# Decoder layer with attention, quantised cross product and gated experts: column sums of the context on GpSimd, row sums and two layernorm applications on ScalarE, product terms added to x ahead of the product

## What is computed

```python
x = x + attn(layernorm(x), Wq, Wk_down, Wv_down, Wk_up, Wv_up, Wo)    # 32 heads, 8 key/value heads, causal
x = x + matmul(fake_quant(layernorm(x), s1, z1), fake_quant(ctx, s2, z2))
x = x + ffn(layernorm(x), A_w, B_w, Wq_w, keys)                        # 64 experts of rank 8, the 16 best gated

def fake_quant(x, s, z):
    return (clip(round(x / s + z), 0, 255) - z) * s
```

## Time and profile before

| | us |
|---|---|
| median of 3 runs | 1156.27 (1155.45 to 1157.93) |
| the profiled execution | 1155.61 |
| its span, first to last instruction | 1153.7 |
| PE busy in the span | 1121.5 (97%) |
| DVE busy | 773.4 (67%) |
| ACT busy | 464.1 (40%) |
| POOL busy | 233.7 (20%) |
| mean granted TensorE clock | 0.994 |

### The profile page before, as it was taken

The page is one execution under the profiler, slowest core; times in us unless marked ns, Lnnn a source line. Parts: engine busy times, 40 slices in busy tenths (PEclk is TensorE's granted clock), DMA queues, the critical chain, the costliest instruction groups (busy, mean ns, idle before and its releaser), DMA issues.

```text
span 1153.7 us, 19016 instructions
## 1 busy us (share of the span) xinstructions
PE 1121.5 (97%) x6632; PEld 603.8 (52%) x6640; DVE 773.4 (67%) x1658; ACT 464.1 (40%) x958; POOL 233.7 (20%) x310
## 2 busy tenths in 40 slices
PE   5999999999999999999999999999999998889997
PEld 4865555555555555555554555455555554445553
DVE  8836766666666666666666666666666677788963
ACT  4436644443444344444444444444434451122211
POOL 4003412221222122212221222122212230000000
PEclk9999999999999999999999999999999999999999
DMA  8004743444344434443444344434443465000001
GB/s 321 24 24 89 177 119 83 102 101 119 82 100 100 118 82 100 100 118 82 100 108 110 82 104 107 115 74 111 100 110 80 104 136 172 1 1 37 19 37 55
DMA packets 189995, 109.73 MB, mean 95 GB/s; under 512 B 170368, under 2 KB 170496, under 8 KB 189952
## 3 DMA queue, kind: packets, MB, share of 16 engines
q1 hardware_dynamic: 189952, 109.15, 37.6%
HBM read 58.80 MB, written 8.39 MB: 58 GB/s over the span
## 4 chain that ended last, share of the span: by engine, by line
PE 92%; DVE 5%; DMA 1%; issue 1%; ACT 1%; POOL 0%; SPq 0%; DVEq 0%; POOLq 0%
PE ps L1177 87%; PE ps L1391 2%; DVE stats L813 1%; PE ps L1407 1%; DVE prob L829 0%; DMA wq_in<-in_a_w 0%; PE ps L1458 0%; DVE rstd L824 0%; DMA prob_t<-prob_s 0%; PE ps L1191 0%; PE ps L1365 0%; DMA x_sb<-in_x 0%; PE ps L1467 0%; POOL prob L554 0%; PE ps L1431 0%
## 5 line engine op out<-in xcount | busy, mean ns | idle before, releaser
L1177 PE MATMUL ps<-wo_sb,o_t 128*128 128x512 f16 x1536 | 352.3, 380 | 3.6 <-DVE x_sb L939 3.6
L1177 PE MATMUL ps<-h_t,wq_sb 128*128 128x512 f16 x1536 | 341.8, 379 | 0.0
L554 POOL TENSOR_SCALAR prob<-prob,row_inv 128x128 f32<-128x128 f32 (+3 forms) x256 | 193.4, 774 | 690.0 <-DVE row_inv L926 690.0
L1177 PEld LDWEIGHTS ps<-h_t,wq_sb 128*128 128x128 f16 x1536 | 150.2, 98 | 179.6
L1177 PEld LDWEIGHTS ps<-wo_sb,o_t 128*128 128x128 f16 x1536 | 148.4, 98 | 173.8 <-DVE x_sb L939 4.1
L699 ACT ACTIVATE prob<-prob,neg_max 128x128 f32<-128x128 f32 (+3 forms) x256 | 140.6, 550 | 208.0 <-DVE neg_max L958 207.9
L939 DVE SCALAR_TENSOR_TENSOR x_sb<-ps,x_sb 128x512 f32<-128x512 f32 x256 | 174.7, 686 | 58.1 <-PE ps L1177 58.1
L805 DVE SCALAR_TENSOR_TENSOR q_t<-ps,q_t 128x512 f16<-128x512 f32 x72 | 49.7, 690 | 200.5 <-ACT q_t L577 200.2
L577 ACT ACTIVATE q_t<-ps 128x512 f16<-128x512 f32 x72 | 43.0, 598 | 274.5 <-PE ps L1177 269.8
L952 DVE CUSTOM_DVE_ANT_0 prob<-ps,mask 128x512 f32<-128x512 f32 (+3 forms) x256 | 112.9, 488 | 6.0
L1177 PE MATMUL ps<-prob_t,v_sb 128*128 128x128 f16 (+2 forms) x960 | 115.3, 273 | 0.3 <-DMA prob_t<-prob_s 0.3
(11 more groups left out here) (111 smaller groups left out, 860.3 us busy)
## 6 DMA issues: line engine op xcount, KB each, us to landing
wq_in<-in_wq SPq DMA_DIRECT2D x32, 512.0 KB, 4.2
wo_in<-in_wo SPq DMA_DIRECT2D x32, 512.0 KB, 3.9
side_in<-in_ctx SPq DMA_DIRECT2D x16, 512.0 KB, 3.9
x_sb<-in_x SPq DMA_DIRECT2D x8, 512.0 KB, 9.6
ctx_quantised<-side_out SPq DMA_DIRECT2D x16, 256.0 KB, 2.4
h_t<-ctx_quantised SPq DMA_DIRECT2D x2, 2048.0 KB, 10.0
out<-x_sb SPq DMA_DIRECT2D x8, 512.0 KB, 2.6
o_t<-in_wdown SPq DMA_DIRECT2D x4, 512.0 KB, 8.8
```

The costliest lines, as they stand in the source:

```text
L554: ins = nc.gpsimd.tensor_scalar(at, at, row_inv[:, u % 2, q:q + 1], S_P, ALU.mult, ALU.mult)
L1177: ins = nc.tensor.matmul(out_, lhs(i), rhs(j), start=start and n == 0, stop=stop and n == 3 * len(pairs) - 1)
```

## The change

- POOL adds every quantised context chunk into `ctx_sum` (128 x 2 x 1024, f16), in units 3 and 7 of each group, behind its normalisation. PE then needs one matmul against `ones` for each half and batch entry, where it had eight. `ctx_sum` is cleared at the start, and the POOL loop is split into two of four groups.
- ACT sums the rows of the integers while it multiplies them by their factor (`sum_rows`); PE's row sums and DVE's L1099 go.
- `fold`: DVE adds column term and row term to x one step ahead of the x product, which is then added straight into x; L1106 and L1111 before.
- Layernorm 3 is applied by ACT from x with a scale and bias per row; layernorm 2's application and the quantisation scale become one ACT pass from x. DVE computes only the scales and biases, 128 x 1 each.
- Two Wo evictions stand ahead of `p_split` in `last_outputs`.

```diff
-        ones = sb("ones", [P, P], BF16)
+        ones = sb("ones", [P, P], F16)
+        ctx_sum = sb("ctx_sum", [P, BATCH, CTX_N], F16)
...
             nc.gpsimd.memset(ones[:, :], 1.0).then_inc(consts, 1)
+            nc.gpsimd.memset(ctx_sum[:, :, :], 0.0).then_inc(ctx_summed, 1)
             pool.wait_ge(consts, 4)
...
+            def add_chunk(g, n, b):
+                pool.wait_ge(side_read, SIDE * g + 2 * n + 1)
+                pool.sem_inc(pool_passed)
+                at = ctx_sum[:, b, :]
+                nc.gpsimd.tensor_tensor(at, at, side_out[:, n, :], ALU.add).then_inc(ctx_summed, 1)
+                pool.wait_ge(ctx_summed, 2 * g + n + 2)
...
                     if u == 1:
                         clip(2 * g)
+                    if u == 3:
+                        add_chunk(g, 0, b)
                     if u == 6:
                         clip(2 * g + 1)
+                    if u == 7:
+                        add_chunk(g, 1, b)
...
             def scale_rows(t):
                 act.wait_ge(ln2_done, t + 1)
-                at = hn[:, t % 2, :]
-                nc.scalar.activation(at, at, ACT.Identity, bias=quant_sb[:, 1:2], scale=inv_scale[:, 0:1])\
-                    .then_inc(x_affine, 1)
+                if t >= 2:
+                    act.wait_ge(x_rounded, t - 1)
+                nc.scalar.activation(hn[:, t % 2, :], x_sb[:, t, :], ACT.Identity, bias=x_bias[:, t:t + 1],
+                                     scale=x_scale[:, 1, t:t + 1]).then_inc(x_affine, 1)
+            def sum_rows(t):
+                act.wait_ge(x_rounded, t + 1)
+                nc.scalar.activation(side_out[:, t % 2, :], x_q[:, t % 2, :], ACT.Identity, scale=shift_scaled[:, 1:2],
+                                     accum_out=row_term[:, t:t + 1]).then_inc(row_summed, 1)
...
             for i in range(-1, TT + STEPS_AHEAD):
+                if 0 <= i and i + 1 < TT:
+                    sum_rows(i + 1)
                 if 0 <= i - 1 < TT:
...
+                if 0 <= i < TT:
+                    act.wait_ge(rstd3_done, i + 1)
+                    if i >= 2:
+                        act.wait_ge(h3_turned, 2 * (i - 1))
+                    nc.scalar.activation(h3[i % 2], x_sb[:, i, :], ACT.Identity, bias=h3_bias[:, i:i + 1],
+                                         scale=rstd1[:, 2, 2 * TT + i:2 * TT + i + 1]).then_inc(h3_done, 1)
                 if 0 <= i + 1 < TT:
...
             def last_outputs():
                 g = KV_HEADS - 1
-                p_split(g, UNITS - 1)
+                for c in range(2 * WO_STEP, 3 * WO_STEP):
+                    if c == 2 * WO_STEP + 2:
+                        p_split(g, UNITS - 1)
+                    wo_add(g, ("wo", 0, 0, c))
                 wo_split(g, 3)
-                for c in range(2 * WO_STEP, 3 * WO_STEP):
-                    wo_add(g, ("wo", 0, 0, c))
...
+            def fold(t):
+                b = t // QT
+                dve.wait_ge(x_affine, t + 1)
+                dve.wait_ge(row_summed, t + 1)
+                dve.wait_ge(column_read, 2 * (b + 1))
+                nc.vector.scalar_tensor_tensor(x_sb[:, t, :], column_term[:, b, :], row_term[:, t:t + 1], x_sb[:, t, :],
+                                               ALU.add, ALU.add).then_inc(x_folded, 1)
...
                     dve.wait_ge(x_done, t + 1)
-                    if t in (0, QT):
-                        dve.wait_ge(column_read, 2 * (b + 1))
+                    dve.wait_ge(x_folded, t + 1)
                     for j in range(2):
                         at = slice(j * HALF, (j + 1) * HALF)
-                        ins = nc.vector.scalar_tensor_tensor(side_in[:, at], ps[:, X_BANK[j], :], both_scales[:, :],
-                                                             column_term[:, b, at], ALU.mult, ALU.add)
+                        ins = nc.vector.scalar_tensor_tensor(x_sb[:, t, at], ps[:, X_BANK[j], :], both_scales[:, :],
+                                                             x_sb[:, t, at], ALU.mult, ALU.add)
...
-                    link(nc.vector.scalar_tensor_tensor(x_sb[:, t, :], side_in[:, :], row_term[:, t:t + 1], x_sb[:, t, :],
-                                                        ALU.add, ALU.add))
...
             def column_sums(b):
-                pe.wait_ge(ctx_loaded[b], 16)
+                pe.wait_ge(ctx_summed, KT * (b + 1) + 1)
                 for j in range(2):
-                    for k in range(KT):
-                        ins = nc.tensor.matmul(ps[:, COLUMN_BANK[b][j], :], ones[:, :], ctx_q[:, b, k, j * HALF:(j + 1) * HALF],
-                                               start=k == 0, stop=k == KT - 1)
-                    ins.then_inc(column_done, 1)
+                    nc.tensor.matmul(ps[:, COLUMN_BANK[b][j], :], ones[:, :], ctx_sum[:, b, j * HALF:(j + 1) * HALF],
+                                     start=True, stop=True).then_inc(column_done, 1)
```

More of the change, by code:

```diff
@@ L325, in decoder_layer @@
         x_affine = sem("x_affine")
+        ctx_summed = sem("ctx_summed")
+        row_summed = sem("row_summed")
+        x_folded = sem("x_folded")
+        rstd3_done = sem("rstd3_done")
         x_qt_copied = sem("x_qt_copied")
@@ L557, in group @@
                         clip(2 * g)
+                    if u == 3:
+                        add_chunk(g, 0, b)
                     if u == 6:
                         clip(2 * g + 1)
-            with pool.Fori(0, KV_HEADS) as g:
-                group(g)
+                    if u == 7:
+                        add_chunk(g, 1, b)
+            with pool.Fori(0, KV_HEADS // 2) as g:
+                group(g, 0)
+            with pool.Fori(KV_HEADS // 2, KV_HEADS) as g:
+                group(g, 1)
             n = TT
@@ L826, in ln_apply @@
                                              ALU.mult, ALU.mult))
-                link(nc.vector.scalar_tensor_tensor(rstd1[:, 2, n:n + 1], rstd1[:, 1, n:n + 1], 1.5, rstd0[:, n:n + 1],
-                                                    ALU.add, ALU.mult))
-                nc.vector.tensor_scalar(dst, x_sb[:, t, :], mean_var[:, n, 0:1], rstd1[:, 2, n:n + 1],
-                                        ALU.subtract, ALU.mult).then_inc(signal, 1)
+                return nc.vector.scalar_tensor_tensor(rstd1[:, 2, n:n + 1], rstd1[:, 1, n:n + 1], 1.5, rstd0[:, n:n + 1],
+                                                      ALU.add, ALU.mult)
             def ln1_apply(t, turn):
@@ L835, in ln1_apply @@
                     dve.wait_ge(ln_turned, 2 * (t - 1))
[L836 removed]
+                link(ln_rstd(0, t, turn))
+                nc.vector.tensor_scalar(hn[:, t % 2, :], x_sb[:, t, :], mean_var[:, t, 0:1], rstd1[:, 2, t:t + 1],
+                                        ALU.subtract, ALU.mult).then_inc(ln_done, 1)
             def ln1_stats(t):
@@ L1067, in quantise_apply @@
             def quantise_apply(t, turn):
-                ln_apply(1, t, turn, hn[:, t % 2, :], ln2_done)
+                n = TT + t
+                link(ln_rstd(1, t, turn))
+                link(nc.vector.scalar_tensor_tensor(x_scale[:, 0, t:t + 1], rstd1[:, 2, n:n + 1], -1.0, inv_scale[:, 0:1],
+                                                    ALU.mult, ALU.mult))
+                nc.vector.tensor_tensor(x_scale[:, 1, t:t + 1], rstd1[:, 2, n:n + 1], inv_scale[:, 0:1], ALU.mult)
+                nc.vector.scalar_tensor_tensor(x_bias[:, t:t + 1], mean_var[:, n, 0:1], x_scale[:, 0, t:t + 1],
+                                               quant_sb[:, 1:2], ALU.mult, ALU.add).then_inc(ln2_done, 1)
             def quantise_end(t):
@@ L1116, in _ @@
                 if i < TT:
-                    if i >= 2:
-                        dve.wait_ge(h3_turned, 2 * (i - 1))
-                    ln_apply(2, i, turn3, h3[i % 2], h3_done)
+                    n = 2 * TT + i
+                    link(ln_rstd(2, i, turn3))
+                    nc.vector.scalar_tensor_tensor(h3_bias[:, i:i + 1], mean_var[:, n, 0:1], -1.0, rstd1[:, 2, n:n + 1],
+                                                   ALU.mult, ALU.mult).then_inc(rstd3_done, 1)
                     if i == 0:
@@ L1124, in _ @@
                     quantise_apply(i + STEPS_AHEAD, turn2)
+                if i + 1 < TT:
+                    fold(i + 1)
                 if 0 <= i - 1 < TT:
@@ L1378, in _ @@
                         pe.wait_ge(gen_read, gen_number(KV_HEADS - 1, ("wo", 1, 0, WO_CHUNKS - 1)))
-                    if t >= 2:
-                        pe.wait_ge(s_copied, t - 1)
-                    for k in range(KT):
-                        ins = nc.tensor.matmul(ps[:, SMALL_BANK, SUM_COL:SUM_COL + 1], x_qt[:, t % 2, k * P:(k + 1) * P],
-                                               ones[:, 0:1], start=k == 0, stop=k == KT - 1)
-                    ins.then_inc(rows_done, 1)
                     if t == 0:
                         pe.wait_ge(column_read, 2)
+                    if t % QT == 0:
+                        pe.wait_ge(ctx_loaded[b], 16)
```

(3 more changed lines are left out.)

25 lines of the change are left out of this document (14 added, 11 removed).

## The result

| | changed | before | ratio |
|---|---|---|---|
| median | 1150.47 us (1149.16 to 1151.57, 4 runs) | 1156.16 us (1155.45 to 1157.93) | 0.9943 [0.9931, 0.9955] |
| profiled execution | 1149.16 us | 1155.61 us | |
| its span | 1147.4 us | 1153.7 us | |

The change makes the kernel 5.7 us faster by the medians; 1150.3 was forecast, with a range of 1147.7 to 1153.3. The profiled execution became 6.45 us faster, its span 6.3 us.

What follows compares the result with a forecast made beforehand. PE was taken to bound the kernel, with waits where the tail fills. Gains of 4.1 (gated z) and 2.0 (row sums) less 0.1 (start) make 6.0 us: 1155.61 becomes 1149.6, median 1150.3 us, range 1147.7 to 1153.3.

Steps and rivals of the forecast that it cites:

- Column sums: Ahead of x product 0 in the tail: two matmuls replace the row of 15 records, so it starts 2.5 us earlier.
- h3: Tail, tile 0: PE starts the transposes of h3 3.2 us earlier in all, after idling 5.8 us.
- Gated z: Tail, PE's second wait: gated z of tile 0 is there 4.1 us earlier; PE still waits some 2.0 us.
- The clock behind it: X product behind the gated z wait: half rate kept at 5.08 us; full speed, 1.7 us less, held as other end.
- rival 1: The second wait no longer costs the clock: 1.7 us more gain, 7.7 in all, 1148.6 us; chance 0.28.
- Row sums: Steps 2 to 7 of the tail: each loses PE's row-sum matmuls, 6 x 0.33 = 2.0 us.
- Adds: POOL's sixteen context adds in the loop fall into DVE's pauses and cost 0 us.
- Start: Kernel start: clearing `ctx_sum` takes 1.8 us and delays the identity; cost taken as 0.1 us, bounds 0 and 0.6.
- Reordering: After the loop: two Wo evictions ahead of the split cost 0 us; the stall of 3.57 us stays.
- Rival 4: The tail's filling steps give nothing; only row sums count, 2.0 us less 0.6 at the start, 1154.9 us; chance 0.08.
- rival 2: ACT paces the filling steps, or longer PE idling costs another half-rate stretch: gain 2 to 4.5 us, about 1153.0; chance 0.15.

Runs made afterwards that it cites:

- e1: The changed kernel with the column sums back on PE as 16 matmuls, POOL's adds and the clearing gone; 1150.57 us.
- e12: e9 with the column sums back on PE and 12 filling matmuls in place of 24; 1143.19 us.
- e9: The changed kernel with 24 filling matmuls before h3's first transposes, last weights A load one unit earlier, first gated z turned behind x product 2; 1140.74 us.
- e11: The changed kernel with unit 3's POOL add ahead of the normalisation instead of behind it; 1150.85 us.
- e5: The changed kernel with layernorm 3 applied by DVE again instead of ACT; 1150.56 us.
- e3: The changed kernel with 24 extra matmuls, result unread, in PE's wait ahead of the first transposes of h3; 1149.14 us.
- e8: The changed kernel run again without edits; 1148.71 us, ratio 0.9943 to the kernel before.
- e10: The changed kernel with the split of the last probabilities back ahead of the two Wo evictions; 1150.65 us.
- e2: The changed kernel with the eight one-column row-sum matmuls per tile added back on PE, result unread; 1151.46 us.
- e6: The changed kernel with the last load of the expert weights A asked for one unit earlier in the last group; 1145.08 us.

## Why the prediction was right

- **Column sums, 2.5 us: 2.3** (2.5 in e1 and e12). Two matmuls for 16, as worked out. DVE's reads ended at 992.29 us. The row of x product 0 starts at 992.76, but it lacks its first record; by e9 to e11 the product starts at T0 + 2.65, 992.55, so the hand-over from DVE to PE that I put at 0.1 us was 0.26.
- **h3, 3.2 us earlier: 3.0** (T0 + 16.16 to 13.12). ACT's pass cost the 0.6 us that were put down (e5). That the fold takes L1111 out of this stretch is seen in the rows only: from DVE's first read of x product 0 to the transposes it takes 6.82 us, 7.52 before. The wait before them was 5.98 us (5.8 forecast). What failed is a step behind it: the clock was low already at the transposes, which took 1.97 us in place of 1.09, so x product 1 came 2.4 us earlier and not 3.2. I had put the half rate at the x product alone. The length of the wait does not explain it: in e1 the transposes took 1.97 us behind 2.96 us, before 1.09 behind 3.66. Filled, the wait costs no clock (e3); what sets the moment of the fall stays open.
- **Gated z, 4.1 us earlier: 3.6,** the same debt with part of it back. The wait was 2.06 us (2.0 forecast).
- **The clock behind it.** Forecast at half rate, 5.08 us; rival 1 had it at full speed. Both happen. The changed kernel and its variants with the same wait (2.06 or 2.07 us) took 3.40 us in four traces (changed, e8; in e10 and e11 the full 16 records took 3.62) and 4.78 to 5.09 us in four (e1, e2, e3, e6). I treated as one unknown what changes from trace to trace. That it is a draw in each execution is likely and not shown: no kernel was seen both ways, e1, e2 and e3 fell on one chip, e10 and e11 did not on another, and only the chip with e6 (fell) and e8 (did not) shows both.
- **Row sums, 2.0 us: 1.2** (six steps of 0.2), the term mis-sized most. The row of L1382 is 0.34 us long, but the eight matmuls hold up what follows by 0.21 us only: a row's length takes in the modelled end of its last matmul, which overlaps with the next. The trace of before shows it at x product 1, which has all its records (1006.99 us):

```profile
1006.78 0.34 PE L1382 MATMUL ps<-ones,q_t 128*128 128x1 bf16 x8
```

No gap hides the rest. In the changed kernel the x product seems to start 0.65 us behind the transposes of z:

```profile
1088.75 0.60 PE L1517 MATMUL ps<-ident,up_in 128*128 128x128 f32 x4
1089.40 3.40 PE L1441 MATMUL ps<-h_t,q_t 128*128 128x512 bf16 x15
```

But its first record is missing. In e10 (16 records) it starts 0.44 us behind them, just where the row sums started before:

```profile
1038.91 0.60 PE L1516 MATMUL ps<-ident,up_in 128*128 128x128 f32 x4
1039.35 3.62 PE L1440 MATMUL ps<-h_t,q_t 128*128 128x512 bf16 x16
```

- **Adds, 0 us: right.** 16 adds of 2.12 us, 14 of them in DVE's pauses and two (the first and the last) beside DVE operations on PSUM, which kept their length; PE is busy for 200.00 of 200 us in the loop. e10 and e11 show the lock, in places where it costs nothing.
- **Start, 0.1 us: right** in size. The clearing took 1.81 us as worked out, and the statistics started at 4.07 us in place of 4.05:

```profile
4.07 1.28 DVE L855 BATCH_NORM_STATS2 stats<-x_sb 128x6 f32<-128x512 f32 x2
```

- **Reordering, 0 us: right** (e10). Rival 4 did not occur, nor did ACT set the pace (rival 2): its copy hid behind the transposes, and it is busy for 6.75 of 17.10 us in a full step. The other half of rival 2, more half rate behind the longer wait, did come, with 0.9 us at the transposes.

So the mechanism was right, and that the median was hit within 0.2 us (1150.3 against 1150.47) is luck. The path's own gain is 4.8 us where 6.0 were summed (0.8 too much for the row sums, 0.5 at gated z, which the clock at the transposes held up), and in the profiled execution the clock behind the second wait gave 1.7 us that were not in the sum. Which share of the executions gets them is not known, and by e8 a second median of the same kernel lies 1.8 us away.

## What to carry to other kernels

Cost removed work by the distance between the starts of its neighbours, not by the duration in its own row, and count the records first: a group that lacks its first one seems to start late. A wait of TensorE may cost more than itself, and whether it does can differ from trace to trace: price such a term as a chance, and read places of a trace, not medians, for effects of 1 to 2 us. Before shortening a producer, look at the wait behind the next one: here 0.6 us bought at h3 came back at the gate, and once both waits were filled DVE's low halves became the bound. And look for work of a later stage that stands in a queue ahead of what is needed now: one load asked for a unit earlier (e6) brought about as much as the whole change.
